# Expert weights of a routed FFN: from a pre-split copy in HBM to an on-chip order, a register load and a split inside the page loop

## The reference

```python
x = x + layernorm(attention(layernorm(x), Wq, Wk, Wv, Wo))   # x: 4 x 512 x 256, 16 heads of 16, rope, causal softmax
x = x + layernorm(ffn(layernorm(x)))
# ffn, on 2048 tokens of width 256:
p = softmax(t @ gate_w.T); w, idx = top_k(p, 4); w = w / w.sum(-1)         # 16 experts
shared = (silu(t @ sg.T) * (t @ su.T)) @ shared_down.T * sigmoid(t @ shared_gate_vec.T)   # width 704
sparse = sum over the 4 chosen experts e of w_e * (silu(t @ g_e.T) * (t @ u_e.T)) @ d_e.T  # width 176
ffn(t) = shared + sparse
```

## Time and profile before

| what | us |
|---|---|
| median of 3 runs | 831.21 (830.64 to 834.49) |
| the profiled execution | 832.64 |
| its span in the profile | 830.7 |
| busy: PE, DVE, ACT, POOL | 603.1 (73%), 442.1 (53%), 349.5 (42%), 414.3 (50%) |
| attention block | 0 to about 413 |
| shared stage | 413.7 to about 570 |
| first gate product of the page loop | 585.11 |
| last adding scatter issued | 795.02 |

### The profile page before, as it was taken

One profiled execution on the slowest core, in us unless ns is written; L12 is line 12 of the kernel. 1 busy time (PEld: TensorE's weight loads), 2 busy tenths in 40 slices (PEclk: granted clock), 3 DMA queues, 4 the chain that ended last, 5 costly groups with the idle time before them and its releaser, 6 DMA issues.

```text
span 830.7 us, 13114 instructions
## 1 busy us (share of the span) xinstructions
PE 603.1 (73%) x4116; PEld 453.9 (55%) x4116; DVE 442.1 (53%) x1105; ACT 349.5 (42%) x656; POOL 414.3 (50%) x501
## 2 busy tenths in 40 slices
PE   0667876877679776787859988693678888888800
PEld 0554534644346343442447867572678888888700
DVE  3769831895349670764377345321344554555428
ACT  1362765174634574224533422231345555555400
POOL 4461876066731866116332675650136666566631
PEclk9979987898889797876989997897799999999955
DMA  8970344024330425013025322224996766667573
GB/s 282 301 226 14 110 133 133 2 86 122 103 96 19 134 80 155 20 37 122 6 75 200 114 101 94 95 107 170 414 292 109 117 114 111 113 109 116 80 198 130
DMA packets 82656, 104.60 MB, mean 126 GB/s; under 512 B 8416, under 2 KB 76448, under 8 KB 80544
## 3 DMA queue, kind: packets, MB, share of 16 engines
q1 hardware_dynamic: 56768, 73.41, 26.8%
q0 software_dynamic: 14448, 19.31, 13.7%
q10 hardware_dynamic: 11376, 11.05, 4.9%
HBM read 48.82 MB, written 54.72 MB: 125 GB/s over the span
## 4 chain that ended last, share of the span: by engine, by line
PE 20%; DMA 10%; DVE 7%; issue 5%; another core or an unknown queue 3%; ACT 2%; POOL 2%; SPq 1%; ACTq 0%; POOLq 0%; DVEq 0%
DMA acc_dram<-yout,xin 8%; PE gate_ps L1804 6%; PE y_ps L1827 3%; PE gate_ps L949 3%; PE y_ps L1770 3%; PE up_ps L949 2%; PE m_ps L1784 1%; SPq L1145 1%; DVE hid L1566 1%; DMA xin<-xs_dram 1%; POOL sw_lo L1195 1%; DVE total L1655 1%; DVE hid_lo L1583 1%; DVE ystats L1642 1%
## 5 line engine op out<-in xcount | busy, mean ns | idle before, releaser
L1234 POOL DMA_INDIRECT acc_dram<-yout,xin x79 | 122.1, 1546 | 118.2 <-ACT yout L1342 68.8
L1804 PE MATMUL gate_ps<-w_all,rxT_hi 128*128 x316 | 83.3, 348 | 34.8 <-issue 21.1
L700 DVE TENSOR_REDUCE nmax<-a_ps 128x2 f32<-128x768 f32 (+3 forms) x88 | 95.2, 1121 | 20.9 <-PE a_ps L848 20.6
L575 ACT ACTIVATE probs<-a_ps 128x1024 f32<-128x1024 f32 (+1 forms) x96 | 81.9, 885 | 51.9 <-PE a_ps L870 51.3
L887 PE MATMUL att_ps<-probs,V 128*32 128x128 f32 (+3 forms) x512 | 58.6, 537 | 46.1 <-POOL probs L506 46.0
L1222 POOL DMA_INDIRECT xs_dram<-xrow,idx x64 | 64.2, 1003 | 39.6 <-issue 18.1
L1619 DVE TENSOR_TENSOR h<-rsilu,gate_ps 128x176 f32<-128x176 f32 x79 | 26.7, 338 | 106.2 <-ACT rsilu L1321 91.4
L846 PE MATMUL a_ps<-KTt,QT 96*128 96x128 bf16 (+3 forms) x256 | 68.8, 341 | 18.4 <-DVE nmax L700 11.9
L506 POOL TENSOR_SCALAR_AFFINE_SELECT probs<-probs 128x256 f32<-128x256 f32 (+1 forms) x96 | 48.6, 508 | 59.4 <-ACT probs L575 58.5
L1804 PEld LDWEIGHTS gate_ps<-w_all,rxT_hi 128*128 128x128 f32 x316 | 56.7, 205 | 36.8 <-issue 36.8
L473 POOL TENSOR_TENSOR rot<-rot,rest 128x512 f32<-128x512 f32 x16 | 21.7, 1357 | 82.0 <-DVE rest L672 82.0
(11 more groups left out here) (250 smaller groups left out, 1599.1 us busy)
## 6 DMA issues: line engine op xcount, KB each, us to landing
w_all<-wsp_dram SPq DMA_DIRECT2D x16, 1088.0 KB, 13.6
xs_dram<-zeros SPq DMA_DIRECT2D x1, 10783.5 KB, 37.9
xin<-xs_dram ACTq DMA_DIRECT2D x79, 136.5 KB, 3.4
raw<-in_wex_dram SPq DMA_DIRECT2D x64, 120.0 KB, 2.2
wsp_dram<-raw_hi SPq DMA_DIRECT2D x64, 120.0 KB, 1.7
wsp_dram<-raw SPq DMA_DIRECT2D x64, 120.0 KB, 1.8
stage<-in_wsh_dram SPq DMA_DIRECT2D x6, 384.0 KB, 3.2
acc_dram<-zeros SPq DMA_DIRECT2D x1, 2176.0 KB, 13.8
```

The costliest lines, as they stand in the source:

```text
L575: nc.scalar.activation(dst, src, ACT.Exp, scale=float(DH) ** -0.5).then_inc(a_act, 1)
L700: nc.vector.tensor_reduce(nmax[:, i, h:h + nh].rearrange("p (b h) -> p b h", h=hb), src, AX.X, ALU.max, negate=True).then_inc(a_dve, 1)
L1234: pool.indirect_dma_start(out=acc[a][:, :], out_offset=bass.IndirectOffsetOnAxis(ap=xin[:, p % XIN, XROW - 1:XROW].bitcast(mybir.dt.uint32 ...
L1804: ins = nc.tensor.matmul(gate_ps[:, p % 2, 0:2 * I], l[:, p % 2, k, :], weights(p, part * SCOLS + k * 2 * I, 2 * I), start=k == 0 and m == ...
```

## The change

1. The copy `wsp`, the pieces, their splits on POOL and their loads and stores on SP are gone from the attention block.
2. DVE compares the first half's page counts of all experts (`earlier`) and orders the experts by them, most pages first; sums over the earlier ones (`ahead`) replace the running sums. In a third part of `first_slots` it writes the order as integers, and SP reads them into 16 registers.
3. SP loads each expert's 128 x 1216 raw weights, 608 KB, through two `stage` buffers; ACT copies the high part (`expert_high`), DVE subtracts twice for the low parts (`expert_low`). The first 3 (`early`, as before) are split at steps 6, 7 and 8 of the shared stage (`EXPERT0`), the other 13 in the page loop, one every second page. PE waits for `w_ready >= min(E, p // 2 + 1)`.
4. `PACE` is 2: scatter n waits for scatter n - 2 to land, and no longer for `down_done`.
5. SP issues the loads of the pages, and between them those of the experts. ACT waits before the page loop for the shared stage's results to be stored.
6. The registers for PE's expert numbers are loaded without a check of their bounds.

```diff
-XIN, YOUT, AHEAD, ACCS = 12, 4, 5, 2
-PIECE, PIECES, PSLOTS = LCOLS // 4, 5, 3
-PACE = 3
+XIN, YOUT, ACCS = 12, 4, 2
+PACE = 2
...
-                if kind == "score":
-                    n = scores
-                    scores += 1
-                    if 2 <= n < E * PIECES + 2:
-                        store_piece(n - 2)
-                    if n < E * PIECES:
-                        load_piece(n)
-                elif kind == "mturn":
...
-                    scores += 1
-                    if 1 < scores <= E * PIECES + 1:
-                        split_piece(scores - 2)
...
-            def expert(e):
-                sp.dma_start(w_all[:, E - 1 - e, :].bitcast(F32), wsp[e]).then_inc(expert_in[e], 16)
+            def expert(k):
+                if k < 2:
+                    sp.wait_ge(slo_done, SH - 1 + k)
+                else:
+                    sp.wait_ge(w_ready, k - 1)
+                load_stage(SH + k, wex_in[bass.ds(which[k], 1)].rearrange("o p n -> (o p) n"), SCOLS)
...
-            for e in range(early):
-                expert(e)
+            sp.wait_ge(order_ready, 1)
+            which = []
+            for k in range(0, E, 8):
+                which.extend(nc.values_load_multi_w_load_instructions(
+                    order_i[0:1, k:k + 8], engines=[mybir.EngineType.SP], min_val=0, max_val=E - 1)[1])
+            for k in range(early):
+                expert(k)
             for i in range(B - 1):
                 store_shared(i)
-            sp.wait_ge(down_done, NSTEP)
+            expert(early)
+            expert(early + 1)
             store_shared(B - 1)
-            for i in range(2):
-                sp.wait_ge(ysh_stored[i], 16 * (B // 2))
-            for e in range(early, E):
-                expert(e)
-            for e in range(E):
-                sp.wait_ge(expert_in[e], 16)
-                sp.nop(nofuse=True).then_inc(w_ready, 1)
+            for i in range(PACE):
+                sp.wait_ge(scattered[i], 16 * (NT * K // PACE))
+            sp.wait_ge(x2_turned, B)
+            for q in range(PAGES):
+                if q >= XIN:
+                    sp.wait_ge(y_added[(q - XIN) % ACCS], 16 * ((q - XIN) // ACCS + 1))
+                sp.dma_start(xin[:, q % XIN, :], xs[q * P:(q + 1) * P, :]).then_inc(xin_in[q % XIN], 16)
+                k = early + 2 + (q - 6) // 2
+                if q >= 6 and q % 2 == 0 and k < E:
+                    expert(k)
...
-                        if k == 0:
-                            pool.wait_ge(down_done, 4 + i)
+                        if n >= PACE:
+                            pool.wait_ge(scattered[n % PACE], 16 * (n // PACE))
...
+            def expert_high(k):
+                n = SH + k
+                act.wait_ge(stage_in[n % 2], 16 * (n // 2 + 1))
+                nc.scalar.copy(w_all[:, E - 1 - k, 0:SCOLS], stage[:, n % 2, :]).then_inc(ehi_done, 1)
...
+                if 0 <= n - EXPERT0 < early:
+                    expert_high(n - EXPERT0)
+            act.wait_ge(down_done, NSTEP)
+            for i in range(2):
+                act.wait_ge(ysh_stored[i], 16 * (B // 2))
...
+                if p >= 0 and p % 2 == 0 and early + p // 2 < E:
+                    expert_high(early + p // 2)
...
-            def running(part):
-                for i in range(4):
-                    old, new = cum[:, i % 2, :], cum[:, 1 - i % 2, :]
-                    link(nc.vector.tensor_tensor(new[:, z:], old[:, z:], old[:, z - 2 ** i:z + E - 2 ** i], ALU.add))
+            def earlier():
+                of_j = pages[:, 0, :].unsqueeze(1).to_broadcast([P, E, E])
+                of_i = pages[:, 0, :].unsqueeze(2).to_broadcast([P, E, E])
+                lower = cst[:, 2 * E + 1:].rearrange("p (a b) -> p a b", b=E)
+                nc.vector.tensor_tensor(before[:], of_j, of_i, ALU.is_gt)
+                link(nc.vector.tensor_tensor(cmp[:], of_j, of_i, ALU.is_equal))
+                link(nc.vector.tensor_tensor(cmp[:], cmp[:], lower, ALU.mult))
+                link(nc.vector.tensor_tensor(before[:], before[:], cmp[:], ALU.add))
+            def ahead(to, counts):
+                link(nc.vector.tensor_tensor(cmp[:], before[:], counts.unsqueeze(1).to_broadcast([P, E, E]), ALU.mult))
+                link(nc.vector.tensor_reduce(to, cmp[:], AX.X, ALU.add))
...
-                link(nc.vector.tensor_copy(cum[:, 0, z:], pages[:, 0, :]))
-                running(0)
-                nc.vector.tensor_copy(ends[:, 0, :], cum[:, 0, z:])
-                link(nc.vector.tensor_tensor(fresh[:], cum[:, 0, z:], pages[:, 0, :], ALU.subtract))
+                earlier()
+                ahead(fresh[:], pages[:, 0, :])
+                nc.vector.tensor_reduce(place[:], before[:], AX.X, ALU.add)
+                link(nc.vector.tensor_reduce(ends[:, 2 * E:], pages[:, 0, :], AX.X, ALU.add))
+                nc.vector.tensor_tensor(ends[:, 0:E], fresh[:], pages[:, 0, :], ALU.add)
...
+                link(nc.vector.tensor_scalar(place[:], place[:], 1.0, None, ALU.add))
+                ones_to = cst[:, E + 1:2 * E + 1]
+                link(nc.vector.tensor_tensor(cmp[:], place[:].unsqueeze(1).to_broadcast([P, E, E]),
+                                             ones_to.unsqueeze(2).to_broadcast([P, E, E]), ALU.is_equal))
+                link(nc.vector.tensor_tensor(cmp[:], cmp[:], ones_to.unsqueeze(1).to_broadcast([P, E, E]), ALU.mult))
+                link(nc.vector.tensor_reduce(order[:], cmp[:], AX.X, ALU.add))
+                nc.vector.tensor_scalar(order_i[:], order[0:1, :], -1.0, None, ALU.add).then_inc(order_ready, 1)
...
+            def expert_low(k):
+                n = SH + k
+                s = E - 1 - k
+                dve.wait_ge(ehi_done, k + 1)
+                nc.vector.tensor_tensor(w_all[64:P, s, LCOLS:SCOLS], stage[64:P, n % 2, LCOLS:SCOLS],
+                                        w_all[64:P, s, LCOLS:SCOLS].bitcast(F32), ALU.subtract)
+                nc.vector.tensor_tensor(w_all[:, s, SCOLS:WCOLS], stage[:, n % 2, 0:LCOLS],
+                                        w_all[:, s, 0:LCOLS].bitcast(F32), ALU.subtract).then_inc(w_ready, 1)
...
+                if p >= 0 and p % 2 == 0 and early + p // 2 < E:
+                    expert_low(early + p // 2)
...
-                        tab[0:1, p:min(p + 8, PAGES)], engines=[mybir.EngineType.PE], min_val=1, max_val=E)[1])
+                        tab[0:1, p:min(p + 8, PAGES)], engines=[mybir.EngineType.PE], min_val=1, max_val=E,
+                        skip_runtime_bounds_check_because="VectorE has bounded the table to 1..E")[1])
...
-                    pe.wait_ge(w_ready, needed[p])
+                    pe.wait_ge(w_ready, min(E, p // 2 + 1))
...
```

126 lines of the change are left out of this document (36 added, 90 removed).

## The result

The kernel after takes 767.33 us in the median of 4 runs (763.29 to 769.43), the kernel before beside it 832.85 (830.64 to 836.25): a ratio of 0.9204 (0.9147 to 0.9262). The forecast was 787.0, 768 to 806. The gain is larger than forecast and just outside the range, and the profile shows that it is a sum of two errors of opposite sign.

A forecast was written before the change was run, and what follows sets the result against it. The prediction took POOL's queue to bound attention outside the maxima, PE's steps the shared stage, and the adding scatters' landing chain the page loop. 830.7 - 39 - 5 = 786.7 us of span, 787 as a median; range 768 to 806.

The forecast's parts named there:

- Splitting leaves the attention block: Attention block: without splits on POOL, PE's waits for masks shrink, -39 us; bounds -20 and -46, all of the waits.
- 149.98 us at 92%: Attention block: PE's 149.98 us of busy time at 92% density take 163 us in place of 202, so 39 less.
- Two scatters under way, 1.8 us: Shared stage: scatters landing in 2.8 us start 1.8 us apart (bounds 0.9 to 2.5); first gate product at 580.0, not 585.1.
- The ordering, early experts and registers: Before and in the shared stage: ordering +1.6 us before the first scatter, register loads 4.7 us, three early experts 4 us, hidden.
- First 26 pages at 2.9 us: Page loop: with a split every second page, 2.9 us a page (2.43 to 3.2), loads hidden; page 26 5 us earlier.
- the ring through splits: First 26 pages: ACT's copy, DVE's subtractions and page work, PE's down product and ACT's `yout` take 5.8 us per two pages.
- SP loads the pages, no bounds check, 0: Page loop: ACT has slack and POOL's backlog covers the register stops, so both changes gain 0.
- Half: Rival, attention block: ACT's exponentials or the list's order stop PE instead, -20 in place of -39: 806 us; chance 0.15.
- splits hidden: Rival, first 26 pages: the splits hide fully, 2.43 us a page, 12.2 us less: 775 us; chance 0.16.
- DVE's subtractions stop POOL: Rival, first 26 pages: subtractions block POOL's generation 1.55 us per two scatters, 3.2 us a page, +8: 795; chance 0.12.
- PE was the limit: Rival, page loop: PE was the limit, so pages take its busy 2.0 us, 21 us less: 766 us; chance 0.05.
- The slower rival, paced scatters: Rival, shared stage: scatters land 5 us after their start, pace 2.9 us, pages 72 us later: 859 us; chance 0.05.

The follow-up runs named there:

- k1: The kernel after, with POOL issuing a 512-byte DMA behind each of 80 masks and waiting for its landing: 851.29 us where before took 813.44.
- d1: The kernel after, with the loads of the first three experts cut to 8 of 1216 columns, splits whole: 760.82 us (0.9326 of before).
- h1: The kernel after, with both the loads and the splits of the 13 late experts cut to 8 columns: 754.31 us (0.9287 of before).
- g2: b2's kernel with the bounds check of PE's register loads back, as in before: 757.73 us where before took 836.11.
- g1: b2's kernel with three accumulators in place of two: 731.64 us where before took 836.11; second run 711.37 us where before took 810.35.
- b1: The kernel after, with three scatters of the shared stage under way in place of two: 780.82 us where before took 835.68.
- f1: b2's kernel with the loads of the 13 late experts cut to 8 of 1216 columns, splits whole: 751.14 us where before took 836.11.
- b2: The kernel after with before's pacing of the shared stage's scatters: 737.12 us where before took 814.27; again 735.09 us where before took 813.44.
- d2: The kernel after, with the splits of the 13 page-loop experts cut to 8 columns, loads whole: 767.32 us (0.9412 of before).

## Why the prediction was wrong, step by step

- **Splitting leaves the attention block, -39: mis-sized, measured -74.3.** This is the step that failed. The mechanism, masks late behind POOL's splits, was right, and the term by waits nearly so: the waits for masks fell by 43.0 us and PE's idle time in the block by 44.6, where 38.5 was reckoned (masks alone cost 3.0 us, not 7.5). What failed is that PE's busy time was taken as given, in "149.98 us at 92%" and in the sum. It was itself inflated by clocks of 0.74 to 0.84 in the earlier trace rows, which the waits had brought about, and fell by 29.7 us for the same products. The sum had no term for the clock, which puts it at nothing without a reason. The bound of -46, "all of them", was no bound, for the same reason. k1 shows cause and effect: waits with no work and next to no traffic behind them take the clock. The Trainium skill, "TensorE: Matmul & The Clock Gate", section "Part 1: The HAM clock gate (the "warmup" mystery)", says that activity releases the throttle. The traces agree: the clock of the second mixed stretch is 1.00, 0.91, 0.86 and 0.79 where the waits for masks are 3.0, 31.4, 46.0 and 50.5 us. By that rule a term for the clock belonged in the sum.
- **Two scatters under way, 1.8 us: measured 1.99.** The landing was well met (2.6 against 2.8). So was the pace of 60 of the 63 steps, 1.77 us. The mean is 1.99 because of the three long steps after landings of 7 to 8.3 us; d1 and h1 show that most of it comes from the experts' loads beside them, to which the forecast gave no effect on the landings. 63 x 0.19 = 12 us is nearly the whole second error. It has the opposite sign and hid a third of the first: that the total missed the range by less than 1 us is owed to this luck, not to the attention term. The stalls went, as thought possible, and gained nothing, as said. The Trainium skill, "DMA: Bandwidth & Descriptors", section "Anatomy of one DMA — SWDGE (gpsimd) path", gives 2.0 us and the bytes over 436 GB/s, an estimate of 2.3 us for 136.5 KB; measured are 2.63 for the last one.
- **The ordering, early experts and registers: right.** The first scatter starts 46.3 us after the end of attention, against 43.8 in before: 2.5 us where 1.6 was said. SP's register loads take 6.6 us where 4.7 was said, an expert's split 1.20 us of ACT and 1.58 of DVE. Loads and splits are hidden by the scatters.
- **First 26 pages at 2.9 us: right number, half the reason.** 2.93 was measured, but the ring through splits was not the limit alone: with the splits gone it stays. The loads were put down as hidden, since PE doesn't wait for them; they delay the landing of others' scatters instead.
- **SP loads the pages, no bounds check, 0: right.** g2 puts the check at 3 us at most.
- **Rivals.** "Half" in attention and "splits hidden" are out: -74.3 us, and 2.93 us a page. "DVE's subtractions stop POOL" was far too large, but it is not nothing: the adding scatter's generation keeps its median of 1547 ns, and two of the 79 take 2.34 and 2.23 us. Both begin while DVE's subtraction of 960 columns runs:

```profile
538.26 1.16 DVE L1531 TENSOR_TENSOR w_all<-stage,w_all 128x960 fp32r<-128x960 f32 x1
538.49 2.34 POOL L1184 DMA_INDIRECT acc_dram<-yout,xin  x1 [0.30 <-issue]
```

  Where the subtraction begins second, neither is longer, and that is nearly always the case; so the price is 1.5 us in 26 pages where the rival had 0.8 us on each page. "PE was the limit" is refuted by g1, though its 766 us would have met the time. The slower rival, paced scatters, was the right place with the wrong size: against before's order of scatters the pacing costs 30 us on a chip without stalls, and some 10 on one with them.

What stays open: what it is that hands PE its instructions only every 1.4 us beside a dense row of scatters, and why not on every chip. No wait of the program shows it, and b1 was not run on a chip where before's order doesn't stall.

## What to carry to other kernels

Where an engine's wait is taken away, look at the granted clock beside the wait: where PE's clock was under 1.00 in that stretch, its busy time shrank too, here by 30 us beside 45 us of idle time. Read a transfer as hidden only when nothing else shares its path: ask whose landing it delays, not only who waits for it. And treat a pacing of DMAs as a change of its own; here it hid a gain of 10 to 30 us behind the gain of 74.

## What the runs showed of the hardware

- Late masks alone cost clock: with a round trip of 512 bytes on POOL behind each of 80 masks and no other work (k1), PE's busy time for the same products was 306.4 us against 271.1 in after, and the clock of the mixed stretches 0.72 to 0.84 against 1.00.
- With indirect scatters starting every 1.28 us, PE's instructions came 1.4 us apart for 26 us in b1. The chain names an unknown queue also in before, f1, g1 and g2, all on chips where before takes 832 to 836 us; in b2 and the second run of g1, on chips with 810 to 814, the same spacing brought no stall. In none of the traces with two under way was there one.
- The same kernel, before, took 810 to 814 us on some chips and 832 to 836 on others; after took 767.3 and 765.6 on two of the latter, and d2, its like, 767.3 on one of the former.
- An indirect scatter of 136 KB lands in 2.6 us, one that adds in 3.8; beside an expert's load of 608 KB landings of 4.9 to 8.3 us stand in after's chain.
- An adding scatter's instruction on POOL took 2.23 and 2.34 us in place of 1.55 where it began during DVE's subtraction of two SBUF tensors, and 1.54 to 1.59 where it began first.
